# Layer norm in the scores' banks, a context chunk prepared later, and a reordered start, in a two-layer attention and FFN kernel

## The reference

```
x = x + xattn0(layernorm(x), ctx)    # 32 query heads on 8 key/value heads, dim 128, rope on q and k
x = x + ffn0(layernorm(x))           # 4-bit weights, gated, inner width 1376
x = x + xattn1(layernorm(x), ctx)    # the same heads, rms norm on q and k
x = x + ffn1(layernorm(x))           # small retrieval module with top-8
```

## Time and profile before

| | |
|---|---|
| median of 3 runs | 2425.37 us (2425.29 to 2427.68) |
| profiled execution | 2425.11 us, its span 2423.3 us |
| PE busy | 2367.6 us, 98% |
| DVE busy | 1625.1 us, 67% |
| ACT busy | 1254.1 us, 52% |
| POOL busy | 1227.8 us, 51% |

### The profile page before, as it was taken

The page is one execution under the profiler, slowest core; times in us unless marked ns, Lnnn a source line. Parts: engine busy times, 40 slices in busy tenths (PEclk is TensorE's granted clock), DMA queues, the critical chain, the costliest instruction groups (busy, mean ns, idle before and its releaser), DMA issues.

```text
span 2423.3 us, 45113 instructions
## 1 busy us (share of the span) xinstructions
PE 2367.6 (98%) x17668; PEld 1295.6 (53%) x17668; DVE 1625.1 (67%) x3133; ACT 1254.1 (52%) x2423; POOL 1227.8 (51%) x983
## 2 busy tenths in 40 slices
PE   8899999999999999999999999999999999999998
PEld 4455555555555555444444655555555555555554
DVE  7977777777777798754444666667666666656566
ACT  7666555656555545433232554555555555544443
POOL 4656566666666666233232445445555555445531
PEclk9999999999999999999999999999999999999999
DMA  6111121212121111011101011122121212221101
GB/s 211 45 45 36 44 53 27 53 27 53 32 53 31 42 40 28 27 44 36 44 11 29 27 31 28 44 53 62 36 62 36 62 36 62 53 43 27 27 14 70
DMA packets 216753, 108.13 MB, mean 45 GB/s; under 512 B 169280, under 2 KB 192480, under 8 KB 216544
## 3 DMA queue, kind: packets, MB, share of 16 engines
q1 hardware_dynamic: 216544, 105.25, 17.5%
HBM read 61.62 MB, written 4.19 MB: 27 GB/s over the span
## 4 chain that ended last, share of the span: by engine, by line
PE 65%; POOL 13%; DVE 11%; issue 5%; ACT 5%; DMA 0%; POOLq 0%; DVEq 0%; SPq 0%; ACTq 0%
PE PB L865 18%; PE PB L817 16%; PE PB L977 9%; PE PB L801 6%; PE PB L994 5%; POOL AR L2711 5%; POOL AR L2716 3%; POOL PSP L2729 2%; PE PB L907 2%; PE PB L842 2%; DVE AR L2128 2%; DVE WB L1933 2%; PE PB L773 2%; POOL AR L2706 1%; ACT JUNK L1330 1%
## 5 line engine op out<-in xcount | busy, mean ns | idle before, releaser
L865 PE MATMUL PB<-WB,AR 128*128 128x512 f16 x3072 | 685.5, 380 | 3.4 <-DVE XTB L1952 1.6
L817 PE MATMUL PB<-XTB,WB 128*128 128x512 f16 x3072 | 679.5, 380 | 1.2 <-DVE XTB L1952 0.7
L865 PEld LDWEIGHTS PB<-WB,AR 128*128 128x128 f16 x3072 | 298.3, 98 | 359.0 <-issue 11.1
L817 PEld LDWEIGHTS PB<-XTB,WB 128*128 128x128 f16 x3072 | 297.5, 98 | 345.3 <-issue 5.6
L2722 POOL TENSOR_TENSOR AR<-AR,SML 128x512 f32<-128x512 f32 x128 | 144.6, 1150 | 318.1 <-DVE SML L2113 318.1
L2143 DVE SCALAR_TENSOR_TENSOR X<-PB,SML,X 128x512 f32<-128x512 f32 x256 | 189.5, 747 | 169.4 <-PE PB L865 163.4
L1490 ACT ACTIVATE AR<-PB 128x512 f16<-128x512 f32 x256 | 132.0, 602 | 248.2 <-PE PB L907 248.2
L2023 DVE TENSOR_TENSOR AR<-PB,AR 128x512 f16<-128x512 f32 x128 | 88.2, 690 | 167.9 <-ACT AR L1453 167.9
L2711 POOL TENSOR_TENSOR AR<-AR,CST 128x512 f32<-128x512 f32 x128 | 183.0, 1430 | 33.9 <-ACT AR L1400 33.9
L977 PE MATMUL PB<-XTB,AR 128*128 128x512 f16 (+1 forms) x864 | 192.5, 379 | 0.0
L1994 DVE TENSOR_TENSOR AR<-AR 128x512 f16<-128x512 f32 x128 | 132.9, 1038 | 74.7 <-ACT AR L1406 74.5
(11 more groups left out here) (273 smaller groups left out, 3776.9 us busy)
## 6 DMA issues: line engine op xcount, KB each, us to landing
STG<-in_wo SPq DMA_DIRECT2D x14, 1024.0 KB
STG<-in_wq SPq DMA_DIRECT2D x13, 1024.0 KB
STG<-in_qw_gu SPq DMA_DIRECT2D x40, 128.0 KB
STG<-in_ctxT SPq DMA_DIRECT2D x4, 1024.0 KB
X<-in_x SPq DMA_DIRECT2D x4, 1024.0 KB, 10.3
out_x<-X SPq DMA_DIRECT2D x16, 256.0 KB, 2.4
STG<-in_wk SPq DMA_DIRECT2D x14, 256.0 KB
STG<-in_wv SPq DMA_DIRECT2D x14, 256.0 KB
```

What stands on the lines that cost most here:

```text
L817: m = pe.do.matmul(b[:, :], wq[x][:, k, h * 128:(h + 1) * 128], XT[y][c][:, k, :], start=n == 0, stop=n == 11)
L865: m = pe.do.matmul(b[:, :], AT[x][:, h, t * 128:(t + 1) * 128], wo[y][:, h, :], start=n == 0, stop=n == 11)
```

## The change

Five edits, all in attention 0 and its preface:

1. `plan_ln`: in attention 0 `ln_turn` and `ln_low` of the first half go from slot 2 to 3, `ln_norm` of the second half from 3 to 4, and its `ln_turn` from 5 to 6.
2. `ln_banks`: norms of units 2, 4 and 30 turn in banks 4 and 5 instead of (2, 3) and (1, 6).
3. Context chunk 2: `peak` goes from slot 0 of unit 2 in bank 6 to slot 2 in bank 4, `scale` from slot 1 to 5, the first `low` from 7 to 8.
4. On ACT `queries_0(u + 1, 3)` now stands ahead of slot 5, in all units of attention 0.
5. Preface: the peak of w(0,1,0) goes behind the fourth head on PE, its squares behind the second head on ACT; on DVE the statistics of chunk 1 are made in two parts, behind heads 0 and 1, and the peak moves behind `queries_0(0, 0)`.

```diff
@@ plan_ln
-            for half, (norm, turn, low) in enumerate(((0, 2, 2), (3, 5, 6))):
+            for half, (norm, turn, low) in enumerate(((0, 3, 3), (4, 6, 6)) if L == 0 else ((0, 2, 2), (3, 5, 6))):
@@ plans
-        plan_at(0, ("c", 2), (1, 9), (2, 0, 6), (2, 1), (2, 7), (2, 9))
+        plan_at(0, ("c", 2), (1, 9), (2, 2, 4), (2, 5), (2, 8), (2, 9))
@@ ln_banks
-        IN_FFN = {(1, 2), (1, 3), (2, 0), (2, 1)}
...
-            return (4, 5) if (i, c) in IN_FFN else ((2, 3), (1, 6))[half]
+            return ((2, 3), (1, 6))[half] if i == 2 and c > 1 else (4, 5)
@@ tensor, preface
-            peak(w(0, 1, 0), 5)
             queries(0, 0, 2)
             queries(0, 0, 3)
+            peak(w(0, 1, 0), 5)
@@ scalar, units
                     if L == 0:
-                        side(0, u, 5)
                         queries_0(u + 1, 3)
                     elif not k_by_dma(1, u + 1):
                         keys_1(u + 1)
-                    for slot in range(5 if L else 6, 10):
+                    for slot in range(5, 10):
                         side(L, u, slot)
@@ scalar, preface
-            squares(w(0, 1, 0))
             turned_q(0, 0)
             turned_q(0, 1)
+            squares(w(0, 1, 0))
             turned_q(0, 2)
@@ vector
-            def ln_stats(i, c):
-                for t in range(4):
+            def ln_sums(i, c, tiles):
+                for t in tiles:
                     dve.wait_ge(*x_made(i, c, t))
                     dve.do.bn_stats(LNS[:, 6 * t:6 * t + 6], X[:, 4 * c + t, :]).then_inc(dv.of(), 1)
+
+            def ln_stats(i, c, tiles=range(4)):
+                ln_sums(i, c, tiles)
@@ vector, preface
-            ln_stats(0, 1)
             turned_q(0, 0)
+            ln_sums(0, 1, (0, 1))
+            turned_q(0, 1)
+            ln_stats(0, 1, (2, 3))
+            turned_q(0, 2)
             mask(0)
-            turned_q(0, 1)
+            queries_0(0, 0)
             peak(w(0, 1, 0), 5)
-            queries_0(0, 0)
-            turned_q(0, 2)
+            turned_q(0, 3)
             queries_0(0, 1)
             scale(w(0, 1, 0))
-            turned_q(0, 3)
             low(w(0, 1, 0), 0)
```

## The result

| | before | changed |
|---|---|---|
| median of 11 runs, us | 2426.03 (2422.81 to 2427.76) | 2430.68 (2426.63 to 2433.30) |
| ratio, 95% interval | | 1.0020 [1.0011, 1.0028] |
| second series, medians, us | 2423.99 (14 runs) | 2430.86 (9 runs), 1.0026 [1.0017, 1.0036] |
| profiled execution, us (span) | 2425.11 (2423.3) | 2433.30 (2431.5) |

The change costs 4.65 us by the medians of the first series, at the edge of what counts as a difference here, and 6.87 by those of the second; both intervals exclude 1. I had forecast 2427.0 with an own range up to 2430 and a full range up to 2431.5: the median of 2430.68 lies in the full range and outside the own one. The profiled execution of the changed kernel is 8.2 longer in span, the longest of its 11 runs; that has to be explained too.

The account below looks back on a forecast made before the run. PE was busy 98% of the span, so only its idle, about 55 us, could be won. Terms -2.7 + 2.4 + 1.3 - 2.35 + 3.0 = +1.65 gave 2427.0 us; own range 2424.5 to 2430, full 2420.0 to 2431.5.

Parts of the forecast that it names:

- Start, -2.7: Before unit 0: ACT free of the last head earlier, a shift of 2.7 us passing whole through units 0 and 1.
- Covered: At the start: the halved clock PE showed after its idle was covered, as ACT was busy throughout.
- Unit 2, +2.4: Unit 2: old waits go, but the shared bank 4 and copies behind ACT's last head cost 2.4 us.
- Unit 4, +1.3: Unit 4: the norm's copies follow ACT's last head, so PE weighs at 202.75 instead of 201.47, 1.3 us later.
- rival B: Halved clock behind the new waits at weighing of units 2 and 4 and fully in unit 30: +4.4, 2431.4 us; chance 0.12.
- Unit 7, -2.35: End of unit 7: last head copied first on ACT, so keys start at 292.05 instead of 294.39, 2.35 us earlier.
- rival D: Unit 7's gain given back at unit 8's wait for the transposed probabilities: +2.35, 2429.4 us; chance 0.07.
- Units with a scale in slot 5, 0: Other units with such a weight: last head POOL-bound near the weighing, change 0, up to 2 us in all.
- Unit 30, +3.0: Unit 30: PE idles 3.5 us before the unpacking; cost 2.3, or 4.0 if the clock halves, taken as 3.0.
- A: New waits in units 2, 4 and 30 don't bite and old waits of units 2 and 4 are won: 2415.1 us; chance 0.12.
- E: The new waits are half as long: -3.3, 2423.7 us; chance 0.10.
- C: The start's shift is lost, POOL's chain lasting as long or DVE late in unit 0: +2.7, 2429.7 us; chance 0.07.

Follow-up runs that it names:

- e12: Kernel of e9 with the start in the order of the kernel before, its filling matmuls kept: 2416.95 us, ratio to the kernel before 0.9971.
- e9: Kernel of e6 plus the start filling of e8, ACT's slot 5 ahead of the last head again in units 8 to 29: 2416.09 us against 2425.06 before.
- e6: Kernel of e4 with the peak of context 2 in bank 2 instead of bank 4: 2417.43 us, ratio to the kernel before 0.9965.
- e5: Kernel before with only the norm's new slots and banks and the later context 2; start and ACT's order as before: 2430.02 us, ratio 1.0021.
- e3: Changed kernel with dummy matmuls filling PE's waits before unit 4's weighing and unit 30's unpacking: 2427.70 us, ratio to the kernel before 1.0013.
- e2: Kernel before with only ACT's last query head moved ahead of slot 5: 2428.45 us, ratio to the kernel before 1.0015.
- e10: Kernel of e9 with chunk 1's statistics moved out of the stretch between the start's heads: 2420.41 us, ratio to the kernel before 0.9980.
- e8: Kernel of e4 with PE's idle at the start filled by dummy matmuls: 2419.83 us, ratio to the kernel before 0.9977.
- e4: Changed kernel with the norm's second copies ahead of the last query head on ACT in units 2, 4, 30: 2420.45 us, ratio to before 0.9982.

## Why the prediction was right or wrong

**Start, -2.7: mis-sized.** 1.7 with the start filled (e12 against e9), 0.46 in the changed kernel as profiled. Two sub-steps failed. I let ACT's last head set the start of unit 1's queries; ACT was free of it at 46.8 (before 48.5; I had 45.7), and then the queries waited 1.48 for the low parts, which I had not followed. The high copies began at 43.20, not 41.95, because DVE's cast of the mask and a subtraction (0.99 and 1.76) stood ahead of the peak, both beside passes of POOL; in the trace of before these took 0.42 and 1.08, and so the replay was too short. From 38.92 to 50.24 DVE had no gap: its work was the chain to follow, not ACT's and POOL's. The Trainium skill's rule that I had quoted and left out of the sum (SBUF — State Buffer, Who interferes with whom) has the one issued first win, and the trace agrees: the same two subtractions took 1.41 when both came ahead of POOL's pass and 2.42 when it was issued between them. Then the halved clock took another 1.2. "Covered" was only half true: the halved 5.28 us head made ACT wait 1.55 us for PE.

**Unit 2, +2.4: right** (+2.50), and mainly for the reasons given: the shared bank 4 (e6 removes it by one number), then copies in series behind POOL's last head. Counted from keys of unit 3 the weighing started at 34.85 (forecast 34.83) and keys of unit 4 at 38.85 (38.73). One step between failed, and by luck it did not show. Behind the 3.70 wait the head ran partly at half clock, and the first output started at 22.74 instead of the forecast 21.13; the wait ahead of the weighing, forecast as 2, shrank to 0.71 and hid it. Without edit 4 it is not hidden, and is nearly all of e5's 1.40.

**Unit 4, +1.3: right as a wait** (1.29 in e3, 1.26 in e5), with 1.5 of halved clock on top in the profiled execution, which was my rival B. But I blamed ACT's new order for it. Each of the two does it alone: the slot (e5, since slot 6 stands behind the last head with or without edit 4) and the order (e2, +1.47).

**Unit 7, -2.35: right** (-2.26 in e3, -2.23 in e2). Nothing was given back in unit 8: rival D is out.

**Units with a scale in slot 5, 0: nearly.** Units 9 to 27 are unchanged, 28 and 29 lost 0.4 together, and e9 gave it back by restoring the order there.

**Unit 30, +3.0: the wait right, the size wrong.** 2.7 without the halving (e3), 5.7 with it; I had put 0.7 for the halving, from the start's 4.44 us head. It hit the whole output and the weighing: 2.55 and 0.3 us, and 0.2 at the unpacking.

**The sum.** With the halving left out: -1.7 + 2.5 + 1.3 - 2.25 + 0.4 + 2.7 = +3.0; as profiled +8.2. The medians' +4.65 and +6.9 lie between. So +1.65 was too low by 1.3, for the start and units 28 and 29, and by 1.7 to 3.9 more for the clock, as far as medians can tell: the part behind the turn-over alone scatters by 4 us.

**The rivals.** A and E are out: the waits were 3.70, 2.42 and 3.36 where I had 3.9, 2.4 and 3.5. C came true in great part in the changed kernel as profiled, where 0.46 of the 2.7 is left. B, at 2431.4, is nearest to both medians: I had given it 0.12, and my own forecast 0.52. It had the right mechanism, and it should have been a term with a size and not only a rival: I set it against one wait of 1.62 us that was harmless. It struck in units 4 and 30, and in unit 2 at a wait where B did not look for it.

## What to carry to other kernels

When a stage moves to a later slot, look up which late-released instruction now stands ahead of it on each engine, and place it into that instruction's idle time: the same copies cost PE 1.3 us (unit 4) and 2.7 us (unit 30) behind the last head, with the halved clock 2.8 and 5.7, and nothing ahead of it. A shared buffer is only as free as its reader is early; the peak's bank was worth 3.7 to 4.9 us. Work taken out where an engine waits anyway wins nothing (e10). Price each new PE wait as long as those here that were followed by half clock (2.42 us and more) with a halved stretch behind it, as a chance, and read the costs by place from the cut timelines, where 0.1 us shows, before asking the medians.

## What the runs showed of the hardware

- The same idle can halve the clock or not. In unit 4 a wait of 2.42 us was followed by 0.52 in the changed kernel twice and by full clock in e5. Waits of 1.6 us in units 2 and 30, and one of 2.08 in e2, were not followed by it; those of 2.85 to 3.70 us in units 2 and 30 in every trace that has them, for a part of the 12 matmuls behind or all of them (3.6 to 5.3 us instead of 2.75). At the start, scores behind two waits close together, of 1.76 and 1.93 us, were halved too (e8). The places filled with dummy matmuls ran at full clock (e3, e8).
- The part behind the turn-over, untouched by any of these kernels, took 1412.7 to 1412.9 us in four traces, 1414.0 to 1415.2 in three and 1416.2 to 1416.9 in seven. What starts one or the other isn't shown. The granted clock goes with it: between 1400 and 1500 us it was 0.95 in the traces of before and of the changed kernel and 0.98 in e4's, and in e4's 1.00 instead of 0.99 from 1900 to 2200.

```profile
1400.00:1500.00 100.00, 93.89 (x784) 54.93 (x783) 58.31 (x118) 51.65 (x115) 51.62 (x44) 0.95 0.16 35
```

```profile
1400.00:1500.00 100.00, 95.25 (x810) 55.61 (x807) 58.26 (x119) 50.52 (x114) 52.84 (x43) 0.98 0.17 35
```

The first is of the kernel before, the second of e4; columns as in the earlier trace rows.
